# Pacing the scatter of tokens by the steps of the shared expert in a two-layer mixture-of-experts kernel

## The reference, cut to what matters

```
logits = einsum('bsd,de->bse', x, router_w)
probs = softmax(logits); top1_val, top1_idx = the largest and its index
hid = einsum('bsd,edh->ebsh', x, up_w) * silu(einsum('bsd,edh->ebsh', x, gate_w))
routed = einsum('ebsh,ehd,ebs->bsd', hid, down_w, mask)     # mask: the expert of each token
shid = (x @ shared_up_w) * silu(x @ shared_gate_w)
shared = shid @ shared_down_w
return ALPHA * top1_val[..., None] * routed + shared
```

## Time and profile before

| what | value |
|---|---|
| three runs | 1076.02, 1077.01 and 1081.60 us, median 1077.01 |
| the profiled execution's own time | 1069.84 us |
| its span, first to last instruction | 1068.1 us |
| mean granted TensorE clock | 0.968 |
| TensorE busy | 957.6 us, 90% |
| VectorE, ScalarE, GpSimd busy | 638.3, 555.4, 452.2 us |
| indirect transfers | 64 of the dispatches and 78 sends |

### The profile page before, as it was taken

One profiled execution on the slowest core, in us unless ns is written; L12 is line 12 of the kernel. 1 busy time (PEld: TensorE's weight loads), 2 busy tenths in 40 slices (PEclk: granted clock), 3 DMA queues, 4 the chain that ended last, 5 costly groups with the idle time before them and its releaser, 6 DMA issues.

```text
span 1068.1 us, 21606 instructions
## 1 busy us (share of the span) xinstructions
PE 957.6 (90%) x7428; PEld 610.4 (57%) x7428; DVE 638.3 (60%) x2100; ACT 555.4 (52%) x1079; POOL 452.2 (42%) x682
## 2 busy tenths in 40 slices
PE   7999999999989989999848998799979958989995
PEld 3566777777643333346316884466646423489994
DVE  3789899998628868726314454777744512344443
ACT  5536676776766455645103554477765201245551
POOL 1146777777517747400742551155530370023331
PEclk9999999999999999999969999999999978999998
DMA  6600000000020000300120243000000011011115
GB/s 213 204 2 3 2 2 3 2 2 3 2 89 0 0 1 0 128 30 1 48 63 23 76 139 88 1 2 2 2 1 1 25 54 33 1 29 46 52 31 170
DMA packets 32602, 42.02 MB, mean 39 GB/s; under 512 B 6960, under 2 KB 26800, under 8 KB 31632
## 3 DMA queue, kind: packets, MB, share of 16 engines
q1 hardware_dynamic: 27952, 31.26, 9.4%
q0 software_dynamic: 4544, 9.38, 2.7%
HBM read 29.16 MB, written 16.66 MB: 43 GB/s over the span
## 4 chain that ended last, share of the span: by engine, by line
PE 76%; DVE 7%; ACT 6%; issue 5%; another core or an unknown queue 3%; DMA 2%; POOL 1%; SPq 0%; DVEq 0%; POOLq 0%; ACTq 0%
PE PS L679 5%; PE PS L431 5%; PE PS L473 4%; PE PS L669 4%; PE PS L662 4%; PE PS L623 4%; PE PS L327 4%; PE PS L336 3%; PE PS L444 3%; PE PS L614 3%; PE PS L616 3%; PE PS L533 2%; PE PS L784 2%; PE PS L424 2%
## 5 line engine op out<-in xcount | busy, mean ns | idle before, releaser
L1609 POOL DMA_INDIRECT token_rows<-xnb,slot_in x78 | 74.6, 956 | 190.7 <-ACT xnb L990 183.4
L890 ACT ACTIVATE pw<-PS 128x384 f32<-128x384 f32 x256 | 111.6, 488 | 71.5 <-PE PS L453 68.8
L1544 POOL TENSOR_SCALAR_AFFINE_SELECT pw<-pw 128x256 f32<-128x256 f32 x256 | 104.6, 432 | 75.6 <-ACT pw L890 73.3
L1148 DVE CUSTOM_DVE_ANT_0 PS<-PS,above 128x256 f32<-128x256 f32 x256 | 115.8, 452 | 23.0 <-PE PS L424 22.8
L1596 POOL TENSOR_TENSOR XS<-XS,N 128x512 f32<-128x512 f32 x64 | 81.1, 1294 | 54.6 <-DVE N L1226 33.8
L431 PE MATMUL PS<-kf,qm 32*128 32x256 f32 x512 | 103.6, 426 | 0.5 <-POOL qm L1553 0.5
L976 ACT ACTIVATE sqb<-PS 128x512 f32<-128x512 f32 x48 | 28.5, 597 | 139.9 <-PE PS L614 87.7
L1400 DVE TENSOR_TENSOR rsb<-sqb,PS 128x256 f32<-128x256 f32 (+1 forms) x78 | 43.3, 555 | 92.6 <-PE PS L669 50.7
L1311 DVE TENSOR_TENSOR rsb<-sqb,PS 128x512 f32<-128x512 f32 x48 | 32.8, 688 | 104.6 <-PE PS L616 49.0
L1566 POOL TENSOR_SCALAR_AFFINE_SELECT pw<-pw 128x256 f32<-128x256 f32 x128 | 55.9, 471 | 69.1 <-ACT pw L1033 69.1
L1150 DVE CUSTOM_DVE_ANT_0 PS<-PS,above 128x128 f32<-128x128 f32 x256 | 84.5, 330 | 0.0
(11 more groups left out here) (211 smaller groups left out, 2377.0 us busy)
## 6 DMA issues: line engine op xcount, KB each, us to landing
sorted_rows<-empty_rows_dram SPq DMA_DIRECT2D x2, 2535.0 KB, 14.6
slot_in<-sorted_rows SPq DMA_DIRECT2D x78, 65.0 KB
N<-token_rows SPq DMA_DIRECT2D x16, 256.0 KB, 5.0
X<-xT_dram SPq DMA_DIRECT2D x8, 256.0 KB, 4.9
ATT<-gate_dram SPq DMA_DIRECT2D x1, 2048.0 KB
XS<-down_dram SPq DMA_DIRECT2D x1, 2048.0 KB
H<-up_dram SPq DMA_DIRECT2D x1, 2048.0 KB
out_dram<-X SPq DMA_DIRECT2D x8, 256.0 KB, 3.0
```

The costliest lines, as they stand in the source:

```text
L890: nc.scalar.activation(pw[:, w % 2, j + n, :], PS[:, A_PST + (2 * v + n) % 3, 0:3 * P], ACT.Exp).then_inc(a_p, 1)
L1148: nc.vector.tensor_tensor_reduce(x[:, 0:SEQ], x[:, 0:SEQ], above[:, :], 1.0, -3e38, ALU.add, ALU.max, mx[:, t // 8 % 2, 1, j, g:g + 1])
L1544: m = nc.gpsimd.affine_select(x[:, :, SEQ * k:SEQ * k + P], x[:, :, SEQ * k:SEQ * k + P], [[0, 2], [1, P]], ALU.is_ge, 0.0, base=0, channe ...
```

## The change

In both dispatches, GpSimd waits before each indirect transfer for a value of `s_hidden` that grows with the number `n` of the transfer. In the second layer it is n * 7 // 8 + 3: transfer `n` waits for step n * 7 // 8, the last one for step 27 of 0 to 31. In the first layer it is n * 2 // 3 + 1, but at most 18: transfers 0 to 2 wait for nothing that is not there, transfer `n` waits for step n * 2 // 3 - 2, and the transfers 26 to 31 all wait for the last step, 15.

```diff
                 pool.wait_ge(q["pos"], 1)
                 pool.wait_ge(r_fill, 32)
                 for n in range(TILES):
+                    pool.wait_ge(q["s_hidden"], n * 7 // 8 + 3 if l else min(n * 2 // 3 + 1, NCH * c["NH"] + 2))
                     nc.gpsimd.indirect_dma_start(sorted_rows[l][:, :], bass.IndirectOffsetOnAxis(pos[:, n:n + 1], 0),
                                                  rows[l][:, n, :], None).then_inc(q["dispatched"], 16)
```

## The result

The changed kernel took 1035.89 us (median of 4 runs, 1035.12 to 1042.69) beside 1079.24 us for the kernel before (4 runs, 1076.02 to 1081.60). The ratio taken over the runs, which is not quite that of the medians, is 0.9622, 95% interval 0.9586 to 0.9658: 3.8% faster. The profiled executions are 34.7 us apart, 1069.84 and 1035.12 us. On another chip the same change made the kernel 0.6% slower; that is the larger finding, and it is told with the experiments.

What follows compares the result with a forecast made beforehand. TensorE, busy 957.6 of 1068.1 us, was taken as the bound, paused by dispatch stalls. First layer -11.3 us and second -22.9 sum to -34.2: 1035.6 us against the profile, 1041 as median, range 1031 to 1060.

Steps and rivals of the forecast that it cites:

- The stall comes from the dispatch, and goes with the waits: Shared expert's steps during both dispatches: a transfer backlog delays them; spreading transfers removes 22.4 us and 22.9 us.
- B: Rival: the first layer's stall stays, the second's goes; 1065 us, about 1054 with half that stall; chance 0.14 with half forms.
- C: Rival: delays come with each transfer or something else there, at any pace; slower, 1088 us; chance 0.08.
- D: Rival: both stalls only shrink, the backlog draining at its own rate; 1065.5 us with half left; chance 0.06.
- The second layer's later end is hidden: Second dispatch's end: slot 0 lands by 910.3 us, TensorE wants it at 915.7, so the later end costs nothing.
- The first layer's tail: First dispatch's end: six transfers after step 15, then the load, delay TensorE's first slot transpose; +8.4 us.
- The clock: Start of the first layer's experts: TensorE runs at a low clock after idling some 10 us; +2.7 us.
- The sum against the profiled execution: Whole kernel: -34.2 us from the profiled 1069.84 us, giving 1035.6 us.
- The median: Whole kernel: runs' median 7.2 us above the profile, a quarter of that taken as stall; 1041 us forecast.
- The step that failed: Drain estimate: the sends, 39 transfers in 65.7 us, show no such wait, so the drain is at least 0.51 per us.
- The prediction's own condition for slower: Whole kernel: slower if the pace removes less than 11.2 of the 45.3 us of stall; slower overall had chance 0.07.
- The rule against it: Shared expert: by the skill page DMA can't delay ScalarE, so thinning transfers gives nothing back; ScalarE's unnamed waits are 48.3 us.

Runs made afterwards that it cites:

- experiment 2: Changed kernel with closer waits, the same fraction in both layers: five steps per eight transfers, 1040.37 us; nine per sixteen, 1050.65 us.
- experiment 1: Changed kernel with waits in one layer alone: second layer only 1048.18 us, first only 1056.81; kernel before 1072.13 on that chip.
- experiment 4: Kernel before with 32 plain copies to consecutive rows replacing the indirect transfers in both dispatches: 1018.32 us issued by GpSimd, 1020.39 by SyncE.
- five per eight: Changed kernel with waits of five steps per eight transfers in both layers: 1040.37 us, ratio 0.9722 to the kernel before.
- nine per sixteen: Changed kernel with waits of nine steps per sixteen transfers in both layers: 1050.65 us, ratio 0.9808 to the kernel before.
- experiment 3: Kernel before plus a GpSimd memset after each dispatch transfer, no waits for steps: 128 columns 1023.95 us, 448 columns 1033.08; kernel before 1021.80.

## Why the prediction was right, step by step

**The stall comes from the dispatch, and goes with the waits: right.** Forecast -22.4 and -22.9 us of steps, measured to 0.0 lost in both. Undoing one layer brought back 19.2 or 19.9 us in that layer alone. Rivals B, C and D are out on these chips: with B or C the steps would have kept gaps of 5 to 13 us, and with D half of them. That it is the pace and not the lock is supported by experiment 2, not proved.

**The second layer's later end is hidden: right.** The last transfer ended at 890.6, and slot 0 was not waited for at 902.54. The term measured -22.88 us.

**The first layer's tail: right in kind, 0.9 us too dear.** From first transfer to slot: forecast 559.5 - 509.3 = 50.2, measured 49.33. From the last transfer's start to the load's it was 2.32 us against 2.30 before, and the slot arrived 1.8 us after that, where I took 2.5.

**The clock: right in size, the place incomplete, the cause not shown.** I charged 2.7 us in the first layer; the row of the table has +1.75 there. I charged nothing in the second layer, where +1.55 came. Together 3.3 against 2.7. But a long pause is not what it takes. With GpSimd's plain copies of experiment 4 TensorE waited 1.93 us for the first layer's first slot, and the clock was 0.53 all the same:

```profile
552.21:556.20 3.99, 3.09 (x14) 2.93 (x15) 1.48 (x6) 0.69 (x2) 0.00 (x0) 0.53 0.00 0
```

In the second layer twelve of the fourteen profiles have 0.71 or 0.72 in the first 6 us of the slots, and 113.3 to 113.6 us to the last send. The other two, the kernel before and the one with five per eight, have 1.00, and 112.0 and 111.9 us. So a slow start costs some 1.5 us there. In the first layer the +1.75 can't be told from the spread of the held-up sends.

**The sum against the profiled execution**: -34.2 forecast, -34.7 measured.

**The median: too high by 5 us.** I took a quarter of the 7.2 us between profile and median as stall. The medians moved by 43.4 us, the profiled executions by 34.7; a forecast with all of it as stall was 1035.6, and the median came out at 1035.89. That this hits it doesn't show that the 7.2 us were stall. The changed kernel's profile is the fastest of its four runs, and the kernel before spreads by 8 to 14 us on the chips without stalls too. The first transfer starts anywhere from 508.1 to 517.6 us in the twelve experiments' profiles, in stages that no edit touches. With four runs each, part of the 43.4 can be luck; the ratio's 3.8% is 41 us, and on the chip of experiment 1 the two layers' ratios add up to 34.8.

**The step that failed, without harm to the number, is the evidence for the pace.** The prediction called the sends 39 transfers in 65.7 us with "no such wait there", and got from them a drain of at least 0.51 per us. The sends were held up too: on chips without stalls they run at 1.43 to 1.45 us, with stalls at 1.72 to 1.75, and the rows showed it only under the names of ordinary releasers. I read the slower pace as what the backlog lets through, 0.57 to 0.58 per us, which is an estimate. With 0.58 in the same working the onset lies at 14 - 17.1 x 0.58 = 4.1, and the first layer's 26 - 38.9 x 0.58 = 3.4 stays just under it. That fits the nearly clean first layer. The closer paces lost 1.8 and 6.8 us there, so the change sits near the edge of what a chip with stalls allows. But a drain of constant rate is not the whole of it: with nine per sixteen, second layer, the last transfer started 43.5 us after the first, which would leave 32 - 43.5 x 0.58 = 6.8, above the onset, and the last ten transfers there delayed nothing.

**What no case of mine held** is a chip without the stall. There the kernel before takes some 1024 us, and the change costs 0.6%; it ran on one such chip only. The prediction's own condition for slower, that less than 11.2 us of stall go, is met there; I had tied it to the transfers and not to the chip.

**The rule against it.** The Trainium skill (SBUF — State Buffer, Who interferes with whom) says that a DMA never contends with a compute engine and that ACT never waits on anyone. For plain copies it held: the same bytes at more than twice the rate delayed no step, on either kind of chip. For indirect ones it did not: ScalarE waited 48.3 us without a named releaser, and none of that in the changed kernel. The page is about the ports of the on-chip memory, and no run shows by what way the transfers delay ScalarE.

**Open:** what the backlog is made of, whether scattered rows are part of it, and why it is there in some places only. That it is the chip is not shown either: none of the experiments' five chips was used twice, and the three without stalls came one after the other in time. The filler of experiment 3, the pace without any lock, did not come to run on a chip with stalls; that the lock itself does nothing rests on the rows named in experiment 2.

## What to carry to other kernels

When instructions of several engines start late with their inputs ready, look at what else is in flight in that stretch, not only at what they wait for, and undo it in one place at a time. A wait that spreads transfers must still leave the last of them time to be hidden: with one transfer left behind the last step the slots began as soon as with six on the chips with stalls, and 5.9 us sooner on the others. And measure a gain like this on several chips before believing it: the same edit was 3.8% faster on one and 0.6% slower on another.

## What the runs showed of the hardware that I had not expected

Two kinds of chip showed, if it is the chip. In three of the six comparisons the kernel before took 1079, 1072 and 1073 us, in the other three 1022, 1024 and 1023. On the first kind 39 indirect transfers of GpSimd of 128 rows come 1.72 to 1.75 us apart, on the second 1.43 to 1.45, beside the same work; GpSimd itself is busy for 0.96 with each. On the first kind, beyond some 14 of them at 1.26 us, ScalarE and VectorE start up to 5 us late. 32 plain transfers from the same queue show nothing of it at 0.53 us each. TensorE's own waits for VectorE's product stayed prompt in the midst of it (553.67 to 553.72).
